# Patch matmuls of a vision tower with 21 of 28 pixels per line in 84 rows and the other seven in partitions 96 to 127

## The reference, cut to what matters

```python
patches = X.reshape(B, C, N_PATCHES, PATCH, N_PATCHES, PATCH)
patches = patches.transpose(0, 2, 4, 1, 3, 5).reshape(B, N_PATCHES * N_PATCHES, IN_D)
tokens = jnp.einsum('bpi,hi->bph', patches, W) + b
```

## Time and profile before

| | us |
|---|---|
| median of 3 runs | 1144.84 (1143.98 to 1146.46) |
| the profiled execution, its own time | 1143.7 |
| its span in the trace | 1141.2 |
| TensorE busy | 1022.0 (90%) |
| ScalarE busy | 640.2 (56%) |
| VectorE busy | 581.3 (51%) |
| GpSimd busy | 383.1 (34%) |
| granted TensorE clock, mean | 0.955 |

### The profile page before, as it was taken

How to read it: one execution, slowest core, us unless ns; L and a number is a source line. 1 busy time by engine, 2 the same in 40 slices (tenths; PEclk the granted TensorE clock), 3 DMA queues, 4 the chain that set the end, 5 groups by cost and what they waited for, 6 DMA issues and landing times.

```text
span 1141.2 us, 20115 instructions
## 1 busy us (share of the span) xinstructions
PE 1022.0 (90%) x4431; PEld 657.4 (58%) x4431; DVE 581.3 (51%) x2099; ACT 640.2 (56%) x1056; POOL 383.1 (34%) x399
## 2 busy tenths in 40 slices
PE   3999999999999999999417999999999759889887
PEld 2345545545455544544316999999999635555554
DVE  3034454344454454344536677777777345555553
ACT  2576666766666666764214555555555436555554
POOL 0001332223333332223370112222222376666661
PEclk9899999999999999999557999999999989999989
DMA  9965665666676565641147677777777222222321
GB/s 241 229 174 161 177 181 175 179 183 184 186 206 179 180 177 175 192 127 37 37 148 237 207 237 238 238 233 237 232 238 221 92 57 78 78 77 81 88 59 37
DMA packets 207860, 185.30 MB, mean 162 GB/s; under 512 B 16893, under 2 KB 182362, under 8 KB 207706
## 3 DMA queue, kind: packets, MB, share of 16 engines
q1 hardware_dynamic: 192256, 155.77, 47.5%
q0 software_dynamic: 12256, 27.81, 7.3%
q10 hardware_dynamic: 3322, 1.44, 0.5%
HBM read 149.10 MB, written 35.85 MB: 162 GB/s over the span
## 4 chain that ended last, share of the span: by engine, by line
PE 72%; POOL 11%; issue 8%; SPq 3%; DVE 3%; DMA 1%; ACT 1%; DVEq 0%; POOLq 0%; ACTq 0%
PE bank L1264 36%; PE bank L1407 12%; PE bank L1399 10%; POOL region L798 9%; PE bank L1269 3%; SPq L376 2%; POOL rstd L732 2%; PE bank L1388 2%; PE bank L1380 1%; PE bank L1471 1%; PE bank L1285 1%; PE bank L1277 1%; PE bank L1299 1%; PE bank L1342 1%; PE bank L1344 1%
## 5 line engine op out<-in xcount | busy, mean ns | idle before, releaser
L1264 PE MATMUL bank<-xf,wp 128*128 128x512 f32 x896 | 427.7, 617 | 5.1 <-ACT xf L540 5.1
L540 ACT ACTIVATE xf<-region 84x1024 f32<-84x1024 f32 x224 | 252.1, 1162 | 48.3 <-DMA region<-in_x 30.3
L1264 PEld LDWEIGHTS bank<-xf,wp 128*128 128x128 f32 x896 | 160.2, 190 | 178.9 <-issue 168.7
L646 ACT ACTIVATE region<-bank,cols 128x256 f32<-128x256 f32 x320 | 135.0, 477 | 130.7 <-PE bank L1399 130.6
L732 POOL TENSOR_TENSOR rstd<-var,neghalf 128x4 f32<-128x4 f32 (+2 forms) x51 | 63.1, 1237 | 386.6 <-DVE var L889 295.4
L1407 PE MATMUL bank<-region 128*128 128x256 f32 x640 | 152.4, 381 | 0.0
L798 POOL DMA_INDIRECT region<-y_rows,gidx x130 | 127.0, 977 | 68.2 <-issue 36.3
L777 POOL DMA_DIRECT2D y_rows<-region x80 | 58.0, 725 | 247.6 <-DVE region L1080 236.6
L748 POOL DMA_INDIRECT z_rows<-z,posg x130 | 128.5, 988 | 37.5 <-issue 37.5
L1399 PE MATMUL bank<-parts 128*128 128x256 f32 x960 | 136.7, 293 | 3.8 <-DVE parts L1095 2.5
L1399 PEld LDWEIGHTS bank<-parts 128*128 128x128 f32 x960 | 122.0, 194 | 4.8 <-issue 4.3
(11 more groups left out here) (172 smaller groups left out, 1211.8 us busy)
## 6 DMA issues: line engine op xcount, KB each, us to landing
region<-in_x SPq DMA_DIRECT2D x384, 196.0 KB
region<-in_L_ffn_ew SPq DMA_DIRECT2D x160, 256.0 KB, 3.1
region<-z_rows SPq DMA_DIRECT2D x80, 128.0 KB, 2.8
y_rows<-region POOLq DMA_DIRECT2D x80, 128.0 KB, 3.5
out<-region SPq DMA_DIRECT2D x65, 64.0 KB
ht_dram<-hT SPq DMA_DIRECT2D x16, 256.0 KB, 3.4
r_dram<-rr SPq DMA_DIRECT2D x16, 256.0 KB, 3.6
region<-ht_dram SPq DMA_DIRECT2D x16, 256.0 KB, 5.2
```

Of the source, the lines that this page charges most:

```text
L540: act.activation(pair_of(i)[0:KROWS], pixels(k, i), ACT.Copy).then_inc(xact_ready, 1)
L646: act.activation(ehT[n % 2][:, c], bank[1 + c][:, 0:EROWS], ACT.Silu, bias=bias[c])\
L1264: ins = pe.matmul(pa[:, :], wp[:, px], pair_of(i)[:, :, j], start=px == 0, stop=px == PATCH - 1)
```

## The change

The 28 pixels of a line are split in 21 main ones (`MAIN`) and seven further ones. The 84 partitions are split in three blocks, 0 to 31, 32 to 63 and 64 to 83 (`BLOCKS`). For block n VectorE copies the seven further pixels of the block's partitions into partitions 96 and on, into the seven columns 7n to 7n + 6 (`move_block`, a copy of 32 or 20 partitions x 512 patches x 7 pixels, inside the pixel buffer). So columns 0 to 20 carry 84 rows of main pixels and up to 32 rows of moved ones, and one patch matmul for each of 21 columns does the whole sum. The weights are laid out to match, with 21 transposes instead of 28. Pairs are 11, the last with one column.

`body` of VectorE now has three moves: block 2 of group g + 1 after `xh`, and blocks 0 and 1 of group g + 2 in the routing, after the rank sums and at the end. ScalarE's copies wait for the moves (`block_moved`) in place of the load: pair 0 for block 0, pair 3 for block 1, pair 7 for block 2. Partitions 84 to 95 and 116 to 127 of both pixel buffers are zeroed once, by four transfers on SyncE (`zero_gaps`): two behind the first pixel load, two ahead of the second. The memsets of `wp` and `xf` go, and one of `wlaid` comes.

```diff
@@ -51,11 +51,14 @@
 ZROWS = E * CAP + SPARE_TILES * EROWS
-PAIRS = PATCH // 2
+MAIN = 21
+BLOCKS = ((0, 32), (32, 64), (64, KROWS))
+EXTRA = PATCH - MAIN
+W_TILES = -(-MAIN // 4)
+FOURTH = 96
+assert MAIN == len(BLOCKS) * EXTRA
+PAIRS = -(-MAIN // 2)
 SLOTS = 5
-
-BY_DVE = ()
-BY_ACT = tuple(i for i in range(PAIRS) if i not in BY_DVE)
 N_LOADS = 18
@@ -140,7 +143,8 @@
         wnat = region[:, XCOLS:XCOLS + CH * PATCH * PATCH].rearrange("h (c y x) -> h c y x", c=CH, y=PATCH)
-        wlaid = region[:, XCOLS + CH * PATCH * PATCH:XCOLS + 2 * CH * PATCH * PATCH].rearrange("h (y c x) -> h y c x", c=CH, x=PATCH)
+        wlaid = region[:, XCOLS + CH * PATCH * PATCH:XCOLS + CH * PATCH * PATCH + P * MAIN]\
+            .rearrange("h (r s) -> h r s", s=MAIN)
         carved = [0]
@@ -339,7 +344,13 @@
-            return xb[k][0:KROWS].rearrange("p (t x) -> p t x", x=PATCH)[:, :, 2 * i:2 * i + 2]
+            return xb[k].rearrange("p (t x) -> p t x", x=PATCH)[:, :, 2 * i:min(2 * i + 2, MAIN)]
+
+        def block_parts(k, n):
+
+            lo, hi = BLOCKS[n]
+            buf = xb[k].rearrange("p (t x) -> p t x", x=PATCH)
+            return buf[FOURTH:FOURTH + hi - lo, :, n * EXTRA:(n + 1) * EXTRA], buf[lo:hi, :, MAIN:PATCH]
@@ -390,11 +401,20 @@
             sp.dma_start(wnat, tok_w.rearrange("h (c y x) -> h c y x", c=CH, y=PATCH)).then_inc(ld_w, 16)
+            def zero_gaps(k):
+
+                for lo, hi in ((KROWS, FOURTH), (FOURTH + BLOCKS[-1][1] - BLOCKS[-1][0], P)):
+                    n = zeros.shape[1]
+                    dst = xb[k][lo:hi].rearrange("p (r c) -> p r c", c=n)
+                    sp.dma_start(dst, zeros[lo:hi, :].unsqueeze(1).to_broadcast([hi - lo, XCOLS // n, n])).then_inc(gap_zeroed[k], 16)
+
             load_x(0, 0)
-            sp.wait_ge(wp_t, PATCH // 4)
+            sp.wait_ge(memset_done, 2)
+            zero_gaps(0)
+            sp.wait_ge(wp_t, W_TILES)
+            zero_gaps(1)
             load_x(1, 1)
-            sp.wait_ge(memset_done, 2)
             for s in range(2, SPARE_TILES):
@@ -517,11 +537,13 @@
             act.wait_ge(ld_w, 16)
-            act.activation(wlaid[:, :, CH - 1], wnat[:, CH - 1], ACT.Copy).then_inc(w_laid, 1)
-            act.wait_ge(pads_zeroed, 2)
-            for b in range(PATCH // 4):
+            act.wait_ge(pads_zeroed, 1)
+            for c in range(1, CH):
+                act.activation(wlaid[:, c:KROWS:CH], wnat[:, c, :, 0:MAIN], ACT.Copy).then_inc(w_laid, 1)
+            for b in range(W_TILES):
+                n = min(4, MAIN - 4 * b)
                 act.wait_ge(wp_t, b + 1)
-                act.activation(wp[0:KROWS, 4 * b:4 * b + 4].rearrange("p x h -> p (x h)"), bank[b][0:KROWS, :], ACT.Copy)\
+                act.activation(wp[:, 4 * b:4 * b + n].rearrange("p x h -> p (x h)"), bank[b][:, 0:n * P], ACT.Copy)\
                    .then_inc(wp_ready, 1)
@@ -532,12 +554,12 @@
-                if lo == 0:
-                    act.wait_ge(x_loaded[k], h * (16 * GIMG * CH) + 16 * GIMG * CH)
                 for i in range(lo, hi):
-                    if i in BY_ACT:
-                        wait_slot(act, g, i)
-                        act.activation(pair_of(i)[0:KROWS], pixels(k, i), ACT.Copy).then_inc(xact_ready, 1)
+                    for n in range(len(BLOCKS)):
+                        if 2 * i <= n * EXTRA < 2 * i + 2:
+                            act.wait_ge(block_moved, g * len(BLOCKS) + (n + 1))
+                    wait_slot(act, g, i)
+                    act.activation(pair_of(i)[:, :, 0:min(2, MAIN - 2 * i)], pixels(k, i), ACT.Copy).then_inc(xact_ready, 1)
@@ -594,19 +616,17 @@
-                high(4, 7)
+                high(4, 6)
                 take_x(g)
-                high(7, 9)
+                high(6, 8)
                 take_s(g)
-                high(9, 10)
+                high(8, 10)
                 take_a(g)
-                high(10, 11)
+                high(10, PAIRS)
                 take_c(g)
                 take_z(g, k, h, nt)
-                high(11, 12)
                 take_r(g, k, h, nt)
                 route_b(g, nt)
-                high(12, 14)
                 high_next(0, 2)
@@ -830,12 +850,18 @@
             dve.memset(rstd2[:, :], 1.0).then_inc(memset_done, 1)
-            for buf in (wp[64:P], xf[64:P]):
-                dve.memset(buf, 0.0).then_inc(pads_zeroed, 1)
-            dve.wait_ge(pads_zeroed, 2)
+            dve.memset(wlaid, 0.0).then_inc(pads_zeroed, 1)
+            dve.wait_ge(pads_zeroed, 1)
             dve.wait_ge(ld_w, 16)
-            for c in range(CH - 1):
-                dve.tensor_copy(wlaid[:, :, c], wnat[:, c]).then_inc(w_laid, 1)
+            dve.tensor_copy(wlaid[:, 0:KROWS:CH], wnat[:, 0, :, 0:MAIN]).then_inc(w_laid, 1)
+            for j, (lo, hi) in enumerate(BLOCKS):
+                for c in range(CH):
+                    first = lo + (c - lo) % CH
+                    rows = len(range(first, hi, CH))
+                    y = (first - c) // CH
+                    at = FOURTH + first - lo
+                    dve.tensor_copy(wlaid[:, at:at + CH * (rows - 1) + 1:CH, j * EXTRA:(j + 1) * EXTRA],
+                                    wnat[:, c, y:y + rows, MAIN:PATCH]).then_inc(w_laid, 1)
             dve.wait_ge(ld_id, 16)
@@ -888,14 +914,14 @@
-            def copy_dve(g, k, h, lo, hi):
-
-                for i in range(lo, hi):
-                    if i in BY_DVE:
-                        if i == BY_DVE[0]:
-                            dve.wait_ge(x_loaded[k], h * (16 * GIMG * CH) + 16 * GIMG * CH)
-                        wait_slot(dve, g, i)
-                        dve.tensor_copy(pair_of(i)[0:KROWS], pixels(k, i)).then_inc(xdve_ready, 1)
+            def move_block(g, k, h, n):
+
+                if n == 0:
+                    if isinstance(g, int) and g < 2:
+                        dve.wait_ge(gap_zeroed[g], 32)
+                    dve.wait_ge(x_loaded[k], h * (16 * GIMG * CH) + 16 * GIMG * CH)
+                dst, src = block_parts(k, n)
+                dve.tensor_copy(dst, src).then_inc(block_moved, 1)
@@ -912,21 +938,23 @@
-                def low(lo, hi):
+                def move(n):
                     if ahead:
-                        copy_dve(r + 1, 1 - k, h_ + k, lo, hi)
+                        move_block(r + 1, 1 - k, h_ + k, n)
+
+                def move_next(n):
+                    if ahead > 1:
+                        move_block(r + 2, k, h_ + 1, n)
...
                     attend_norm(r, k, link, settle)
-                low(3, 4)
-                low(4, 5)
                 if attn:
...
                     normalise(xh, h[k], mv, rstd1, GT).then_inc(xh_ready, 1)
-                low(5, 6)
+                move(2)
                 dve.wait_ge(t4_done, r + 1)
...
@@ -1007,7 +1031,7 @@
                 pp_step = link(dve.tensor_tensor(pk, pk, oh[:, 0:nk], ALU.mult))
-                low(12, 13)
+                move_next(0)
                 settle(gsm_step)
@@ -1015,13 +1039,13 @@
                 dve.tensor_copy(posg[k][:, 0:nk], posf[:, 0:nk]).then_inc(pos_ready, 1)
-                low(13, 14)
-                if ahead > 1:
-                    copy_dve(r + 2, k, h_ + 1, 0, 3)
+                move_next(1)
                 assert m[0] == A_STEPS * attn + R_STEPS, m[0]
-            copy_dve(0, 0, 0, 0, PAIRS)
-            copy_dve(1, 1, 0, 0, 3)
+            for j in range(len(BLOCKS)):
+                move_block(0, 0, 0, j)
+            for j in range(2):
+                move_block(1, 1, 0, j)
             body(0, 0, 0, nt=1)
@@ -1244,24 +1268,19 @@
             pe.wait_ge(memset_done, 2)
-            pe.wait_ge(w_laid, CH)
-            for px in range(PATCH):
-                ins = pe.transpose(bank[px // 4][0:KROWS, (px % 4) * P:(px % 4 + 1) * P],
-                                   wlaid[:, :, :, px].rearrange("h y c -> h (y c)"), ident)
-                if px % 4 == 3:
+            pe.wait_ge(w_laid, CH + CH * len(BLOCKS))
+            for s in range(MAIN):
+                ins = pe.transpose(bank[s // 4][:, (s % 4) * P:(s % 4 + 1) * P], wlaid[:, :, s], ident)
+                if s % 4 == 3 or s == MAIN - 1:
                     ins.then_inc(wp_t, 1)
...
                 for i in range(lo, hi):
-                    if i in BY_ACT:
-                        pe.wait_ge(xact_ready, g * len(BY_ACT) + (BY_ACT.index(i) + 1))
-                    else:
-                        pe.wait_ge(xdve_ready, g * len(BY_DVE) + (BY_DVE.index(i) + 1))
-                    for j in range(2):
-                        px = 2 * i + j
-                        ins = pe.matmul(pa[:, :], wp[:, px], pair_of(i)[:, :, j], start=px == 0, stop=px == PATCH - 1)
+                    pe.wait_ge(xact_ready, g * PAIRS + (i + 1))
+                    for s in range(2 * i, min(2 * i + 2, MAIN)):
+                        ins = pe.matmul(pa[:, :], wp[:, s], pair_of(i)[:, :, s % 2], start=s == 0, stop=s == MAIN - 1)
                     ins.then_inc(xpair_used, 1)
```

(3 more changed lines are left out.)

11 lines of the change are left out of this document (4 added, 7 removed).

## The result

| | before | after |
|---|---|---|
| median of 4 runs each, us | 1145.28 | 1169.54 (1168.47 to 1170.66) |
| ratio, 95% interval | | 1.0212 (1.0194 to 1.0230) |
| span of the profiled execution, us | 1141.2 | 1166.8 |
| granted TensorE clock, mean | 0.955 | 0.913 |
| TensorE busy, us | 1022.0 | 953.1 |

The kernel is 2.1% slower; forecast was 1145, range 1113 to 1163, so the time lies above the range. The last two rows divide the 25.6 us between the spans: 32.6 are lost before the second group (122.49 - 89.88), 7.7 are gained from there to the last group (448.54 before, 440.86 after), 0.7 are lost behind it (602.8 and 603.4).

A forecast was written before the change was run, and what follows sets the result against it. TensorE was taken to bound the kernel. Shorter work (25.7 us), a new wait (4.2) and clock loss (2.1) left the period at 32.0; with the second group 6.1 us late the sum was +1.4, so 1145, range 1113 to 1163.

The forecast's parts named there:

- the start: Before the second group: zeros on SyncE take 12.5 us ahead of the second pixel load; second group at 96.0, 6.1 late.
- The move: On VectorE: each copy of 3584 elements per partition takes 2.06 us, the low end; high end 3.94.
- The rival at 3.94: VectorE moves at the slow pace, 3.94 us each: wait 6.1, clock falls, 33 us more, 1177; chance 0.10.
- Moves 2 and 1 hidden: On VectorE: move 2 delays `a_bd` 0.1 us, inside its 0.9 spare; move 1 ends near 29.8, before L921 at 30.6.
- The wait of TensorE: End of each group: TensorE waits 4.2 us while move 0, two ScalarE copies and the patch take finish.
- TensorE's work: Steady group: seven of 28 patch matmuls go, 6.3 us, leaving 25.7 us of work on TensorE.
- The clock loss: After each wait TensorE returns at the low clock, costing 2.1 us a group; bounds 0 and 2.45.
- The rival in which the clock holds: The wait seldom or never lowers TensorE's clock: 28 us less, 1116; chance 0.16.
- The period: Steady group: 29.9 us of chain plus 2.1 of clock loss gives 32.0, the same as before.
- The load: Pixel load of 28.6 us lands 2.4 us before move 0, not the bound; as a rival 1155, chance 0.04.
- own range: Likeliest case, whole kernel: wait, clock loss and start varied together give 1132 to 1160 us; chance 0.70.

The follow-up runs named there:

- e9: Kernel before plus only the four transfers of zeros on SyncE, ScalarE's first copies of the first two groups waiting for them: 1178.94 us, ratio 1.0302.
- e1: Changed kernel with the zeros written by VectorE memsets in pieces ahead of each image's pixel transfers, instead of four transfers: 1146.33 us, ratio 1.0008 to the kernel before.
- e5: Changed kernel with zeros written by GpSimd memsets and ScalarE taking finished patches and `w` ahead of all copies: 1091.44 us, ratio 0.9519 to the kernel before.
- e3: Changed kernel with ScalarE's take of finished patches ahead of the copies of pairs 0 and 1: 1131.39 us, ratio 0.9879 to the kernel before.
- e2: Changed kernel with four idle matmuls filling TensorE's wait at the end of each group with patches ahead: 1147.61 us, ratio 1.0020 to the kernel before.
- e8: e5 with move 0 placed ahead of VectorE's wait for the rank sums: 1086.44 us, ratio 0.9481 to the kernel before.

## Why the prediction was wrong

**The step that failed** is the start, and in it one term: "by runs the zeros are worth 12 of them, 11.0 us, by bytes 12.6. I take 12.5. Bounds: half of it (source and target both on the chip) and twice it." Measured: 38.9 us on the queue (e9 alone 38.1), outside even the upper bound of 25. The rest of the start's sum held: the zeros took 26.4 us more than forecast, and the second group came 26.5 us late, at 122.49 instead of 96.0, which by itself turns 1145.1 into 1171.6. The pixel transfers gave the price of a run and of a byte at 28 partitions a transfer; the zeros go to 12. The nearest row could have been read by partition: 224 runs of 896 bytes in 0.92 us are 218 GB/s over 28 partitions, 7.8 each, and 12 partitions at that pace 93 GB/s, that is 29 us; measured were 6.1 a partition. I had no reason to leave that reading out of the bounds, though it too falls short of 38.9, and it takes the pixel transfers to run one after the other, which no row shows. What the runs put in place of the term is its measured size: e9 adds the four transfers alone and gets the late start whole, e1 and e5 take them away and the second group starts at 98.67 (with the memsets' own delay) and at 83.97. Why they are this slow stays open.

**The steps that held:**
- The move: forecast 2.06 us, measured 2.02. The rival at 3.94 fell.
- Moves 2 and 1 hidden: yes. VectorE still waits 1.27 us behind move 1, and in the group from 312.24 to 343.60 TensorE has no idle time but the one at its start.
- The wait of TensorE: forecast 4.2, measured 3.97, released by ScalarE's take. e3 shows its cause.
- TensorE's work: forecast 25.7, e2's row 25.8.
- The clock loss: forecast 2.1, measured 1.94 (31.71 - 25.8 - 3.97), and 1.75 by e2's period. Those are means over 13 periods, of which the first lost nothing; the bound of 2.45 was a little short for a single period (32.70 less e2's 29.96 is 2.7). The rival in which the clock holds fell, in twelve periods of 13. It would have been right in e2, where the wait is filled; there the period is still 29.96, since the chain behind move 0 is as long.
- The period: forecast 32.0, measured 31.71. From the second to the last group the forecast was 443.8, measured 440.86.
- The load: not the bound (move 0 without a wait at 338.65), until e8, where it holds move 0 back.

So the sum was right for the steady groups, and wrong by a factor of three in one term of the start. No rival covered that term with a case of its own, and the range gave it 12 us at most. The own range was also narrower than its terms: all of them at their ends give 1127 to 1168, not 1132 to 1160.

## What to carry to other kernels

A transfer of an unseen form is priced by bytes, by runs and by partitions. Even the dearest of the three (29 us) was short of the 38.9 measured here, so such a transfer is best run by itself first, as e9 does. Transfers that run once, at the start, stand in the time but for the slack that was there if the first loads queue behind them: of 38.9 us on the queue 32.6 reached the second group. Issue time on the queue is not the price of a transfer: look at the next transfers' issue and at GB/s by window. Where a change takes matmuls away, ask what they covered: here the six behind the ranks covered what VectorE and ScalarE do before the next group can start. Taking the finished patches ahead of the new chain of move and copies gave 1.2% by itself (e3), taking the zeros off the queue by VectorE only made up the loss (e1), and both with the zeros on GpSimd gave 4.8% (e5), with move 0 earlier 5.2% (e8, 1146.12 to 1086.44 on one chip).
